# Seven block products instead of eight in the down projection of 29 of 64 groups

## The chip, the cores and the metric

The kernel runs on one core of one Trainium2 chip. The metric is device time in microseconds of one execution of the whole program; a version's time is the median of its runs. The engines are named as the profile names them: PE is TensorE (PEld its weight loads), DVE is VectorE, ACT is ScalarE, POOL is GpSimd, SP is SyncE, which only issues transfers here.

## The reference

Two layers of gated cross attention and feed-forward act on x of 2 x 1024 tokens with 256 features. The part that the change touches is the feed-forward part of the first layer, a sum over 8 experts of a gated MLP with 1024 hidden features:

```
x = x + tanh(g_xattn[0]) * attention(layernorm(x), ctx, ctx, W, b)
def expert_step(acc, w):
    wg, wu, wd = w
    h = silu(x @ wg) * (x @ wu)        # x: 2048 x 256, wg and wu: 256 x 1024
    return acc + h @ wd                # wd: 1024 x 256
x = x + tanh(g_ffn[0]) * scan(expert_step, 0, (Wg, Wu, Wd))(layernorm(x))
x = x + tanh(g_xattn[1]) * masked_attention(layernorm(x), ctx, mask, ...)
x = x + tanh(g_ffn[1]) * routed_experts(layernorm(x), ...)
```

All tensors are float32. The second attention has 8 heads, and the last layer sends each token to one of 8 experts with 256 places each.

## The kernel before

The feed-forward stage takes the time from about 75 to 1044 us of a span of 1275 us. Before it stands the first attention, behind it the second attention and the routed experts.

**Tiling.** The 8 x 1024 hidden features are cut into 32 quarters of 256 features, the 2048 tokens into two pairs of chunks of 2 x 512 tokens. A group is one quarter for one pair of chunks, so there are 64 groups. From group 4 on the even groups (pair 0) and the odd groups (pair 1) alternate on the same quarter's weights. Everything is kept transposed: features on the 128 partitions, 512 tokens along the row. A group is thus a product of matrices of 2 x 2 blocks: two blocks of 128 features by two chunks of 512 tokens.

**Gate and up.** For each of the two, the 2 x 2 block product is done by seven block products in place of eight (Strassen and Winograd's form): `product1` to `product7`, with sums of weight blocks and of activation blocks made ahead of time. The weight sums are made by POOL for each quarter in `split_hi` and `split_lo`.

**Three matmuls for one product.** Every block product keeps nearly float32 accuracy by splitting both factors into a high part, rounded to the format that PE reads in one pass, and a low part, the rest. `three` (three matmuls, L1124 to L1126) does high x high, low x high and high x low. The activation's high parts are copies on ACT (`hi_part`, L821), the low parts subtractions on DVE (`lo_part`, L1742). The down weights are split by POOL (`split`, L546 and L548).

**Down.** A group's hidden blocks are called 11, 12, 21, 22 (feature block, chunk). `down(n, part)` has eight parts, each a `three`; two parts accumulate in one bank and form a turn, and DVE adds each of the four turns to the running sum `acc` in SBUF (`add_up`, L1756). So a group has 14 + 8 = 22 block products, 66 matmuls, and four additions.

**Order.** The order is written out by hand on each engine. PE runs in iteration n the 14 products of group n and, between them, the parts of `down` for group n-1, and part 7 of group n-2. DVE's loop has for each group four sums that complete gate and up (`sum_22`, `sum_12`), four products silu(gate) x up (`hid_psum` L1725 and `hid_sum` L1734: the names hid11, hid21, hid22, hid12), four low parts and four additions, 16 instructions. `hid_sum` and `lo_part` read two operands in SBUF, the others one in PSUM and one in SBUF. ACT copies halves out of PSUM, does the silu and the high parts, 14 instructions. POOL does once per quarter, so once per two groups, the ten instructions that split gate and up weights (L516 to L540) and two for the down weights; it starts on a quarter when the last product of the group before (`p4_ps["u"]`) has set the buffers free. SP reloads raw weights behind POOL.

## Time and profile before

| | us |
|---|---|
| median of 3 runs | 1281.11 |
| lowest, highest | 1277.74, 1281.66 |
| the profiled execution's own time | 1277.14 |
| span of its profile | 1275.4 |
| PE busy in the span | 1248.7 |
| DVE busy | 908.1 |
| ACT busy | 643.5 |
| POOL busy | 557.7 |

Busy times are sums over instructions with overlaps taken out. One matmul is shown with 0.39 us, but matmuls are pipelined: the distance of two starts is what one costs. On DVE the distance of two starts in a row is likewise shorter than what one instruction is shown with. A row of the timeline that merges several instructions (x2, x4) gives the time from the start of the first to the end of the last.

### The profile page before, as it was taken

To read this page: it belongs to the slowest core of one execution; us is meant where nothing else is said; L and a number is where in the kernel's file an instruction comes from. 1 tells how busy PE (TensorE), PEld (TensorE's weight loads), DVE (VectorE), ACT (ScalarE), POOL (GpSimd) and SP (SyncE) were. 2 spreads that over 40 slices of the span, in tenths; PEclk is the share of its full clock that TensorE was granted. 3 is DMA by queue.
4 is the path that set the end of the run, shared out by engine and by line. 5 is a ranking of instruction groups with operands and counts; after the bars stand their busy time and mean duration, and the time that the engine had idled before them with its cause. 6 is when DMAs were issued, how large, how long until landed. Compare 5 with 4: busy or idle time off the path is not lost.

```text
span 1275.4 us, 17854 instructions
## 1 busy us (share of the span) xinstructions
PE 1248.7 (98%) x6236; PEld 1008.2 (79%) x6236; DVE 908.1 (71%) x1663; ACT 643.5 (50%) x1369; POOL 557.7 (44%) x545
## 2 busy tenths in 40 slices
PE   7999999999999999999999999999999999999998
PEld 5778888888888888888888888888888877787775
DVE  5897767777777677777777777777777775677546
ACT  2465554554555555545445555555554445545543
POOL 3644654444444444444444444444444016544435
PEclk9999999999999999999999999999999999999999
DMA  4100300000000000011000000000000130000131
GB/s 136 47 4 1 117 26 25 25 26 25 25 25 25 25 25 25 26 37 39 25 26 25 26 25 25 26 25 26 26 25 1 50 116 1 18 22 15 34 96 62
DMA packets 41640, 44.04 MB, mean 35 GB/s; under 512 B 4159, under 2 KB 40063, under 8 KB 41423
## 3 DMA queue, kind: packets, MB, share of 16 engines
...
## 4 chain that ended last, share of the span: by engine, by line
PE 90%; DVE 4%; ACT 3%; issue 1%; POOL 1%; DMA 0%; POOLq 0%; ACTq 0%; DVEq 0%
PE bank L1125 26%; PE bank L1124 26%; PE bank L1126 25%; ACT PC L867 2%; PE bank L1338 2%; PE bank L1329 2%; PE bank L1491 1%; PE bank L1508 1%; DVE nmC L1812 1%; PE bank L1441 1%; PE bank L1313 1%; PE bank L1263 1%; PE bank L1268 1%; PE bank L1264 1%; PE bank L1030 1%
## 5 line engine op out<-in xcount | busy, mean ns | idle before, releaser
L1124 PE MATMUL bank<-xop_hi,w_hi 128*128 128x512 f32 x896 | 350.9, 392 | 1.2 <-ACT half_g L798 1.2
L1125 PE MATMUL bank<-xop_lo,w_hi 128*128 128x512 f32 x896 | 351.7, 393 | 0.0
L1126 PE MATMUL bank<-xop_hi,w_lo 128*128 128x512 f32 x896 | 350.9, 392 | 0.0
L1756 DVE TENSOR_TENSOR acc<-bank,acc 128x512 f32<-128x512 f32 x248 | 170.9, 689 | 119.7 <-PE bank L1126 119.5
L1742 DVE TENSOR_TENSOR hid_lo<-hid,hid_hi 128x512 fp32r<-128x512 f32 x256 | 213.8, 856 | 34.7 <-ACT hid_hi L821 34.6
L1124 PE MATMUL bank<-hid_hi,wd_hi 128*128 128x512 f32 x512 | 202.5, 395 | 0.6 <-DVE hid_lo L1742 0.6
L1125 PE MATMUL bank<-hid_lo,wd_hi 128*128 128x512 f32 x512 | 203.0, 396 | 0.0
L1124 PEld LDWEIGHTS bank<-xop_hi,w_hi 128*128 128x128 f32 x896 | 168.2, 188 | 42.2 <-ACT half_g L798 1.5
L1126 PE MATMUL bank<-hid_hi,wd_lo 128*128 128x512 f32 x512 | 201.4, 393 | 0.0
L1125 PEld LDWEIGHTS bank<-xop_lo,w_hi 128*128 128x128 f32 x896 | 168.2, 188 | 38.3
L1126 PEld LDWEIGHTS bank<-xop_hi,w_lo 128*128 128x128 f32 x896 | 168.1, 188 | 37.3
L806 ACT ACTIVATE s<-bank 128x512 f32<-128x512 f32 x128 | 78.1, 611 | 176.1 <-PE bank L1126 176.1
L821 ACT CAST hid_hi<-hid 128x512 fp32r<-128x512 f32 x256 | 157.8, 624 | 1.9 <-DVE hid L1734 1.9
L782 ACT COPY bank<-bank 128x512 f32<-128x512 f32 x128 | 73.0, 570 | 123.5 <-PE bank L1126 123.5
L516 POOL TENSOR_TENSOR w_raw<-raw_gu 128x256 f32<-128x256 f32 x32 | 24.1, 753 | 250.3 <-PE bank L1126 250.3
L546 POOL CAST wd_hi<-raw_d 128x512 fp32r<-128x512 f32 x32 | 19.6, 613 | 234.3 <-PE bank L1126 234.3
L1126 PEld LDWEIGHTS bank<-hid_hi,wd_lo 128*128 128x128 f32 x512 | 96.4, 188 | 22.8
L1124 PEld LDWEIGHTS bank<-hid_hi,wd_hi 128*128 128x128 f32 x512 | 96.1, 188 | 22.9 <-DVE hid_lo L1742 1.0
L1125 PEld LDWEIGHTS bank<-hid_lo,wd_hi 128*128 128x128 f32 x512 | 96.0, 187 | 21.1
L1725 DVE TENSOR_TENSOR hid<-bank,s 128x512 f32<-128x512 f32 x128 | 87.8, 686 | 19.7 <-PE bank L1126 19.7
L812 ACT ACTIVATE half_g<-half_g 128x512 f32<-128x512 f32 x128 | 81.2, 635 | 20.6 <-DVE half_g L1715 19.5
L536 POOL TENSOR_TENSOR w_lo<-w_raw,w_hi 128x1024 fp32r<-128x1024 f32 x32 | 86.5, 2704 | 4.0 <-DVE xnA L1578 1.6
...
## 6 DMA issues: line engine op xcount, KB each, us to landing
...
slots<-empty_row SPq DMA_DIRECT2D x1, 2080.0 KB, 10.8
...
x_res<-in_x_dram SPq DMA_DIRECT2D x4, 512.0 KB, 5.1
...
out_dram<-x_res SPq DMA_DIRECT2D x3, 512.0 KB
```

The lines of the kernel that those rows point to most:

```text
L536: nc.gpsimd.tensor_tensor(out=lo[:, :, W_S1:W_S4 + 1], in0=s[:, :, W_S1:W_S4 + 1], in1=hi[:, :, W_S1:W_S4 + 1].bitcast(F32), op=ALU.subtract)
L782: nc.scalar.copy(bank[FORK_BANK[X]][:], bank[SUM_BANK[X]][:]).then_inc(forked[X], 1)
L806: nc.scalar.activation(out[:], ps[:], ACT.Silu).then_inc(silu_ready[h], 1)
L812: nc.scalar.activation(half["g"][:], half["g"][:], ACT.Silu).then_inc(silu_ready[h], 1)
L821: nc.scalar.copy(hid_hi[n % 2][h][:], hid[h][:]).then_inc(hi_ready[h], 1)
L867: ins = nc.scalar.activation(PC[j % 2][:, h, :], bank[SIM[h // HH * 2 + h % 2]][:, a * KEYS:(a + 1) * KEYS], ACT.Exp, bias=nmC[j % 2][:, h ...
L1124: mm(ps, w, a, start=start, stop=False, skip_group_check=True)
L1125: mm(ps, w, a_low, start=False, stop=False, skip_group_check=True)
L1126: return mm(ps, w_low, a, start=False, stop=True, skip_group_check=True)
L1725: nc.vector.tensor_tensor(out=hid[h][:], in0=ps[:], in1=s[:], op=ALU.mult).then_inc(hid_ready[h], 1)
L1742: nc.vector.tensor_tensor(out=hid_lo[n % 2][h][:], in0=hid[h][:], in1=hid_hi[n % 2][h][:].bitcast(F32), op=ALU.subtract).then_inc(lo_ready ...
L1756: nc.vector.tensor_tensor(out=to, in0=ps, in1=to, op=ALU.add).then_inc(acc_added, 1)
```

## The change

In 29 groups (pair 0, quarters 2 to 30: groups 4, 6, ... 60) the down projection is also done by seven block products, called M1 to M7 by the kernel. For that:

- POOL makes for each such quarter four sums of 128 x 128 blocks of the down weights and splits them (`split_down_sums`: six instructions, put ahead of `split_hi`), and for each such group four sums of hidden blocks T3, T1, T2, T4 (`hid_sums`: four 128 x 512 subtractions, put between `split_lo` and `split_down`). `split_down_sums` waits for the sixth product of the group two before.
- ACT makes the high parts of 11, 21, 22 and of the four T, seven instead of four; DVE makes as many low parts, and adds seven products instead of four turns: M2, M3 and M4 to blocks of `acc`, M1, M5, M6 and M7 to accumulators of their own.
- PE does each M as one `three` into one bank, so 21 matmuls instead of 24, in the order M1, M3, M2, M7, M5, M6, M4, in the places of `down`'s parts; one place (step 4) stays empty. M4 stands in the next iteration, as part 7 did.
- Once, after group 60, POOL joins the four accumulators into `acc` by eight additions (`join_products`), before DVE may add group 62.
- The new tiles lie where x_res (the residual, 16 KB per partition) was. x_res is therefore written to DRAM (x_mid) once, early in the stage, and read back in four transfers after group 60; the residual additions wait for them.

The diff, cut to its core (`add_up`, `hi_part`, `lo_part` and the waits on counters are otherwise adapted to the new counts by `turns_before` and `splits`):

```diff
+        def seven(n):
+            return inside(n) and pair(n) == 0 and 2 <= quarter(n) <= NQ - 2
+        def turns(n):
+            return len(M_ORDER) if seven(n) else 4
+        def turns_before(n):
+            return sum(turns(m) for m in range(n))
+        def sevens_before(n):
+            return sum(seven(m) for m in range(n))
+        def splits(n, h):
+            return n + 1 - (sevens_before(n + 1) if h == "12" else 0)
+        M_ORDER = ("M1", "M3", "M2", "M7", "M5", "M6", "M4")
+        T_ORDER = ("T3", "T1", "T2", "T4")
...
+                if q == 2:
+                    sp.wait_ge(a_ln2, NC)
+                    sp.dma_start(x_mid, x_res[:]).then_inc(x_kept, 16)
...
+            def split_down_sums(q):
+                d, S1, S2, S3, S4 = raw_d[q % 2], 0, 1, 2, 3
+                f0, f1 = slice(0, P), slice(P, 2 * P)
+                if q == 2:
+                    pool.wait_ge(x_kept, X_KEPT + 16)
+                else:
+                    pool.wait_ge(down_ps, turns_before(PAIRS * (q - 1)) + M_ORDER.index("M6") + 1)
+                nc.gpsimd.tensor_tensor(out=wds_raw[:, S1], in0=d[:, 0, f1], in1=d[:, 1, f1], op=ALU.add)
+                own_step(nc.gpsimd.tensor_tensor(out=wds_raw[:, S3], in0=d[:, 0, f0], in1=d[:, 0, f1], op=ALU.subtract))
+                own_wait()
+                own_step(nc.gpsimd.tensor_tensor(out=wds_raw[:, S2], in0=wds_raw[:, S1], in1=d[:, 0, f0], op=ALU.subtract))
+                own_wait()
+                own_step(nc.gpsimd.tensor_tensor(out=wds_raw[:, S4], in0=d[:, 1, f0], in1=wds_raw[:, S2], op=ALU.subtract))
+                own_wait()
+                own_step(nc.gpsimd.tensor_copy(wds_hi[:], wds_raw[:]))
+                own_wait()
+                nc.gpsimd.tensor_tensor(out=wds_lo[:], in0=wds_raw[:], in1=wds_hi[:].bitcast(F32),
+                                        op=ALU.subtract).then_inc(wds_ready, 1)
+            def hid_sums(n):
+                k = len(T_ORDER) * sevens_before(n)
+                pool.wait_ge(down_ps, turns_before(n - 1))
+                pool.wait_ge(hid_ready["22"], n + 1)
+                pool.wait_ge(hid_ready["12"], n + 1)
+                nc.gpsimd.tensor_tensor(out=t_raw["T3"][:], in0=hid["22"][:], in1=hid["12"][:], op=ALU.subtract).then_inc(t_ready, 1)
+                nc.gpsimd.tensor_tensor(out=t_raw["T1"][:], in0=hid["12"][:], in1=hid["11"][:], op=ALU.subtract).then_inc(t_ready, 1)
+                pool.wait_ge(t_ready, k + 2)
+                nc.gpsimd.tensor_tensor(out=t_raw["T2"][:], in0=hid["22"][:], in1=t_raw["T1"][:], op=ALU.subtract).then_inc(t_ready, 1)
+                pool.wait_ge(t_ready, k + 3)
+                pool.wait_ge(hid_ready["21"], n + 1)
+                nc.gpsimd.tensor_tensor(out=t_raw["T4"][:], in0=hid["21"][:], in1=t_raw["T2"][:], op=ALU.subtract).then_inc(t_ready, 1)
+            def join_products(n):
+                c11, c12 = (acc[:, 0, t * CH:(t + 1) * CH] for t in range(2))
+                c21, c22 = (acc[:, 1, t * CH:(t + 1) * CH] for t in range(2))
+                m1, m5, m6, m7 = (m_acc[i][:] for i in ("M1", "M5", "M6", "M7"))
+                def add(to, a):
+                    return nc.gpsimd.tensor_tensor(out=to, in0=to, in1=a, op=ALU.add)
+                pool.wait_ge(acc_added, turns_before(n + 1))
+                own_step(add(m6, m1))
+                add(c11, m1)
+                own_wait()
+                add(m7, m6)
+                own_step(add(c12, m6))
+                own_wait()
+                add(c21, m7)
+                own_step(add(c22, m7))
+                own_wait()
+                add(c12, m5)
+                add(c22, m5).then_inc(joined, 1)
...
             for q in range(2, NQ):
-                split(q)
+                n = PAIRS * (q - 1)
+                if seven(n):
+                    split_down_sums(q - 1)
+                split_hi(q)
+                split_lo(q)
+                if seven(n):
+                    hid_sums(n)
+                split_down(q)
+            join_products(n)
...
+            def t_hi_part(n, i):
+                if not seven(n):
+                    return
+                act.wait_ge(t_ready, len(T_ORDER) * sevens_before(n) + T_ORDER.index(i) + 1)
+                nc.scalar.copy(t_hi[i][:], t_raw[i][:]).then_inc(t_hi_ready, 1)
             for n in range(GROUPS + 1):
                 fork(n, "g")
@@ -826,13 +958,20 @@
                 fork(n, "u")
                 if n == 0:
                     x_raw_out(2)
+                if seven(n - 1):
+                    hi_part(n - 1, "21")
+                    t_hi_part(n - 1, "T3")
                 keep_u2(n, "g")
-                hi_part(n - 1, "21")
+                if not seven(n - 1):
+                    hi_part(n - 1, "21")
+                t_hi_part(n - 1, "T1")
                 if n == 1:
                     x_hi_first(1)
                 keep_p5(n, "g")
                 keep_p5(n, "u")
+                t_hi_part(n - 1, "T2")
                 silu_psum(n, "11", s11, bank[SUM_BANK["g"]], p2_ps)
+                t_hi_part(n - 1, "T4")
...
+            def down_seven(n, m):
+                i, turn = quarter(n) % 2, turns_before(n) + M_ORDER.index(m)
+                whole_hi, whole_lo = wd_hi[i][:], wd_lo[i][:]
+                f0, f1 = slice(0, P), slice(P, 2 * P)
+                own, at = (hid_hi[n % 2], hid_lo[n % 2]), (t_hi, t_lo)
+                w, w_low, (hi, lo), h = {
+                    "M1": (whole_hi[:, 0, f0], whole_lo[:, 0, f0], own, "11"),
+                    "M2": (whole_hi[:, 1, f0], whole_lo[:, 1, f0], own, "21"),
+                    "M3": (wds_hi[:, 3], wds_lo[:, 3], own, "22"),
+                    "M4": (whole_hi[:, 1, f1], whole_lo[:, 1, f1], at, "T4"),
+                    "M5": (wds_hi[:, 0], wds_lo[:, 0], at, "T1"),
+                    "M6": (wds_hi[:, 1], wds_lo[:, 1], at, "T2"),
+                    "M7": (wds_hi[:, 2], wds_lo[:, 2], at, "T3")}[m]
+                if m == "M1":
+                    pe.wait_ge(wds_ready, sevens_before(n) + 1)
+                    pe.wait_ge(lo_ready["11"], splits(n, "11"))
+                elif m == "M6":
+                    pe.wait_ge(t_lo_ready, T_LO_READY + len(T_ORDER) * sevens_before(n) + T_ORDER.index("T2") + 1)
+                else:
+                    pe.wait_ge(acc_added, turn - 1)
+                three(bank[DOWN_BANK[turn % 2]][:], w, w_low, hi[h][:], lo[h][:], True).then_inc(down_ps, 1)
...
+            def down_step(n, step):
+                if not seven(n):
+                    down(n, step)
+                elif step != 4:
+                    down_seven(n, M_ORDER[step if step < 4 else step - 1])
...
+            def t_lo_part(n, i):
+                dve.wait_ge(t_hi_ready, T_HI + len(T_ORDER) * sevens_before(n) + T_ORDER.index(i) + 1)
+                if i in ("T1", "T2"):
+                    dve.wait_ge(t_ready, len(T_ORDER) * sevens_before(n) + T_ORDER.index(i) + 2)
+                nc.vector.tensor_tensor(out=t_lo[i][:], in0=t_raw[i][:], in1=t_hi[i][:].bitcast(F32),
+                                        op=ALU.subtract).then_inc(t_lo_ready, 1)
...
+                if n == GROUPS - 2 and part == 0:
+                    dve.wait_ge(joined, JOINED + 1)
...
+            def add_seven(n, m):
+                turn = turns_before(n) + M_ORDER.index(m)
+                own_block = {"M2": (0, 0), "M3": (0, 1), "M4": (1, 0)}
+                f, t = own_block.get(m, (0, 0))
+                to = acc[:, f, t * CH:(t + 1) * CH] if m in own_block else m_acc[m][:]
+                ps = bank[DOWN_BANK[turn % 2]][:]
+                dve.wait_ge(down_ps, turn + 1)
+                if m not in own_block and sevens_before(n) == 0:
+                    nc.vector.tensor_copy(to, ps).then_inc(acc_added, 1)
+                else:
+                    nc.vector.tensor_tensor(out=to, in0=ps, in1=to, op=ALU.add).then_inc(acc_added, 1)
...
+                if seven(n):
+                    group_of_seven(n)
+                elif seven(n - 1):
+                    group_behind_seven(n)
+                else:
+                    group(n)
```

DVE, around the end of an even group and the start of the odd one behind it. Names: hidXY are the products silu(gate) x up, hid_lo their low parts, half22 and half12 the sums that complete gate and up, acc the running sum, m_acc the new accumulators. Before:

```order
L1742 TENSOR_TENSOR hid_lo12_0_132<-hid12_126,hid_hi12_0_128 128x512
L1742 TENSOR_TENSOR hid_lo22_0_134<-hid22_165,hid_hi22_0_130 128x512
L1756 TENSOR_TENSOR acc_143<-bank7,acc_143 128x512
L1742 TENSOR_TENSOR hid_lo11_0_131<-hid11_125,hid_hi11_0_127 128x512
L1742 TENSOR_TENSOR hid_lo21_0_133<-hid21_164,hid_hi21_0_129 128x512
L1756 TENSOR_TENSOR acc_143<-bank6,acc_143 128x512
L1707 TENSOR_TENSOR half22_g_123<-bank1,half22_g_123 128x512
L1715 TENSOR_TENSOR half12_g_121<-bank2,half12_g_121 128x512
L1725 TENSOR_TENSOR hid11_125<-bank3,s11_119 128x512
```

Between the low part of block 21 and the first sum of the next group stood one addition. The same place now, for a group of seven (hid_lo12_0 holds the low part of T3 here):

```order
L1911 TENSOR_TENSOR hid_lo11_0_131<-hid11_125,hid_hi11_0_127 128x512
L1935 TENSOR_TENSOR acc_159<-bank7,acc_159 128x512
L1911 TENSOR_TENSOR hid_lo21_0_133<-hid21_180,hid_hi21_0_129 128x512
L1919 TENSOR_TENSOR hid_lo12_0_132<-t_rawT3_155,hid_hi12_0_128 128x512
L1948 TENSOR_TENSOR m_accM1_156<-bank6,m_accM1_156 128x512
L1919 TENSOR_TENSOR t_loT1_148<-t_rawT1_147,t_hiT1_146 128x512
L1876 TENSOR_TENSOR half22_g_123<-bank1,half22_g_123 128x512
L1948 TENSOR_TENSOR acc_159<-bank7,acc_159 128x512
L1884 TENSOR_TENSOR half12_g_121<-bank2,half12_g_121 128x512
L1894 TENSOR_TENSOR hid11_125<-bank3,s11_119 128x512
L1948 TENSOR_TENSOR acc_159<-bank6,acc_159 128x512
```

Two more instructions stand ahead of the first sum of the next group, and additions of products stand between the sums; over the two groups DVE has 38 instructions where it had 32.

POOL, once per quarter, from the first instruction for the weights of a quarter on. Before:

```order
L516 TENSOR_TENSOR w_raw0_151<-raw_gu0_160 128x2x128
L517 TENSOR_TENSOR w_raw0_151<-raw_gu0_160 128x2x128
L519 CAST w_hi0_150<-raw_gu0_160 128x2x256
L521 TENSOR_TENSOR w_raw0_151<-w_raw0_151,raw_gu0_160 128x2x128
L523 CAST w_hi0_150<-raw_gu0_160 128x2x128
L525 TENSOR_TENSOR w_raw0_151<-raw_gu0_160,w_raw0_151 128x2x128
L528 CAST w_hi0_150<-w_raw0_151 128x2x512
L536 TENSOR_TENSOR w_lo0_152<-w_raw0_151,w_hi0_150 128x2x512
L538 TENSOR_TENSOR w_lo0_152<-raw_gu0_160,w_hi0_150 128x2x256
L540 TENSOR_TENSOR w_lo0_152<-raw_gu0_160,w_hi0_150 128x2x128
L546 CAST wd_hi0_153<-raw_d0_162 128x512
L548 TENSOR_TENSOR wd_lo0_154<-raw_d0_162,wd_hi0_153 128x512
```

After the change the sums of the down weights stand ahead of L516's successor (L571), and after the last of the ten:

```order
L621 TENSOR_TENSOR wds_raw_144<-raw_d1_179,wds_raw_144 128x128
L623 CAST wds_hi_143<-wds_raw_144 128x512
L625 TENSOR_TENSOR wds_lo_145<-wds_raw_144,wds_hi_143 128x512
L571 TENSOR_TENSOR w_raw0_167<-raw_gu0_176 128x2x128
...
L592 TENSOR_TENSOR w_lo0_168<-raw_gu0_176,w_hi0_166 128x2x128
L634 TENSOR_TENSOR t_rawT3_155<-hid22_181,hid12_126 128x512
L635 TENSOR_TENSOR t_rawT1_147<-hid12_126,hid11_125 128x512
L637 TENSOR_TENSOR t_rawT2_150<-hid22_181,t_rawT1_147 128x512
L640 TENSOR_TENSOR t_rawT4_153<-hid21_180,t_rawT2_150 128x512
L603 CAST wd_hi0_169<-raw_d0_178 128x512
```

POOL has 22 instructions per quarter instead of 12, and the T sums, which the hidden blocks of the same group must wait for, stand behind 16 of them.

## Rows read from the trace of the kernel before

**Rows 1.** The page: busy times and shares, and the chain that ended last.
```profile
span 1275.4 us, 17854 instructions
PE 1248.7 (98%) x6236; PEld 1008.2 (79%) x6236; DVE 908.1 (71%) x1663; ACT 643.5 (50%) x1369; POOL 557.7 (44%) x545
PE 90%; DVE 4%; ACT 3%; issue 1%; POOL 1%; DMA 0%; POOLq 0%; ACTq 0%; DVEq 0%
```

**Rows 2.** Timeline of PE (start us, us): the first matmul of two even iterations.
```profile
610.75 0.39 PE L1124 MATMUL bank<-xop_hi,w_hi 128*128 128x512 f32 x1
...
641.21 0.39 PE L1124 MATMUL bank<-xop_hi,w_hi 128*128 128x512 f32 x1
```

**Rows 3.** Busy time by stretch: PE, PEld, DVE, ACT, POOL, clock, DMA share, GB/s.
```profile
610.75:641.22 30.47, 30.47 (x134) 24.79 (x133) 21.97 (x33) 15.50 (x28) 13.22 (x13) 1.00 0.08 27
1044.00:1275.40 231.40, 217.60 (x1715) 171.40 (x1713) 145.77 (x477) 116.18 (x393) 105.91 (x94) 1.00 0.12 41
```

**Rows 4.** Who waited for whom in the span: us in total, times, longest.
```profile
POOL w_raw L516 <- PE bank L1126: 250.3, 29, 8.7
POOL wd_hi L546 <- PE bank L1126: 234.3, 29, 8.3
```

**Rows 5.** Timeline of DVE in an odd iteration and the even one behind it.
```profile
608.04 0.68 DVE L1715 TENSOR_TENSOR half_u<-bank,half_u 128x512 f32<-128x512 f32 x1
608.64 1.28 DVE L1734 TENSOR_TENSOR hid<-half_u,half_g 128x512 f32<-128x512 f32 x2
...
623.28 0.68 DVE L1715 TENSOR_TENSOR half_u<-bank,half_u 128x512 f32<-128x512 f32 x1
```

**Rows 6.** Timeline of POOL in quarters 3 and 4.
```profile
129.34 1.19 POOL L516 TENSOR_TENSOR w_raw<-raw_gu 128x256 f32<-128x256 f32 x1
130.49 0.74 POOL L517 TENSOR_TENSOR w_raw<-raw_gu 128x256 f32<-128x256 f32 x1
131.18 0.61 POOL L519 CAST w_hi<-raw_gu 128x512 fp32r<-128x512 f32 x1
...
134.72 2.40 POOL L536 TENSOR_TENSOR w_lo<-w_raw,w_hi 128x1024 fp32r<-128x1024 f32 x1
137.08 1.74 POOL L538 TENSOR_TENSOR w_lo<-raw_gu,w_hi 128x512 fp32r<-128x512 f32 x1
138.78 1.19 POOL L540 TENSOR_TENSOR w_lo<-raw_gu,w_hi 128x256 fp32r<-128x256 f32 x1
...
176.37 1.30 POOL L548 TENSOR_TENSOR wd_lo<-raw_d,wd_hi 128x512 fp32r<-128x512 f32 x1
```

**Rows 7.** Timeline of DVE in the same and an earlier stretch.
```profile
80.41 6.13 DVE L1742 TENSOR_TENSOR hid_lo<-hid,hid_hi 128x512 fp32r<-128x512 f32 x4
...
95.17 3.05 DVE L1742 TENSOR_TENSOR hid_lo<-hid,hid_hi 128x512 fp32r<-128x512 f32 x2 [1.57 <-ACT hid_hi L821]
...
136.41 2.96 DVE L1734 TENSOR_TENSOR hid<-half_u,half_g 128x512 f32<-128x512 f32 x2
139.29 0.68 DVE L1725 TENSOR_TENSOR hid<-bank,s 128x512 f32<-128x512 f32 x1
```

**Rows 8.** POOL's float32 subtractions of 128x512 beside them, merged.
```profile
78.44 7.55 POOL L380 TENSOR_TENSOR xop_raw<-xop_raw 128x512 f32<-128x512 f32 x4 [3.79 <-ACT xop_raw L731]
```

**Rows 9.** Groups by line: busy us, mean ns, idle before.
```profile
L1742 DVE TENSOR_TENSOR hid_lo<-hid,hid_hi 128x512 fp32r<-128x512 f32 x256 | 213.8, 856 | 34.7 <-ACT hid_hi L821 34.6
L821 ACT CAST hid_hi<-hid 128x512 fp32r<-128x512 f32 x256 | 157.8, 624 | 1.9 <-DVE hid L1734 1.9
L546 POOL CAST wd_hi<-raw_d 128x512 fp32r<-128x512 f32 x32 | 19.6, 613 | 234.3 <-PE bank L1126 234.3
```

**Rows 10.** The line of the low parts: duration ns min/median/max.
```profile
L1742 DVE TENSOR_TENSOR hid_lo<-hid,hid_hi x256: 672/684/1786, 80.4 to 1040.4; 128x512 fp32r<-128x512 f32 x128
```

**Rows 11.** DMA issues of the page: KB each, us to landing.
```profile
slots<-empty_row SPq DMA_DIRECT2D x1, 2080.0 KB, 10.8
x_res<-in_x_dram SPq DMA_DIRECT2D x4, 512.0 KB, 5.1
```

167 lines of the change are left out of this document (122 added, 45 removed).

## The prediction, made before the change was timed

> **What bounds the kernel now.** I read the page first: PE is busy in 98% of the span and holds 90% of the chain that ended last, DVE is at 71%, POOL at 44% [rows 1]. Then the timeline of PE: two iterations (an even group and the odd one behind it, a pair from here on) take 641.21 - 610.75 = 30.46 us for 132 matmuls, 0.2308 us each and 0.692 us for a `three`, with no gap [rows 2]. The windows say what else a pair holds: DVE 21.97 us, ACT 15.50, POOL 13.22, clock 1.00 [rows 3]. So PE bounds the stage and a matmul taken away is time gained, as long as nobody else needs more than PE. The waits show the slack of POOL, 17 us per pair: 8.6 before a quarter's first sum and 8.1 before the down weights [rows 4]. DVE has 30.5 - 22.0 = 8.5 us of slack. The last view is the timeline of DVE beside that of POOL, because the change loads just these two, and there stands what decides.
>
> A DVE instruction of 128x512 costs 0.60 us in a row (608.04 to 608.64), and two hid products 1.28 [rows 5]. With POOL at work beside them it is otherwise. The same two products took 2.96 us at 136.41: POOL was in L536 from 134.72 to 137.12; the first product waited for its end, then POOL's L538, shown with 1.74 us instead of the 1.30 of a free 128x512 subtraction, waited 0.45 for the product, and the second product waited for L538 [rows 6, 7]. They alternate, an instruction of the one for an instruction of the other. Four low parts beside POOL's subtractions took 6.13 us, 1.53 each, and two took 3.05 [rows 7]. The instruction with one operand in PSUM at 139.29 took 0.68, undisturbed [rows 7], though POOL's L540 ran from 138.78 to 139.97 [rows 6]. So only DVE instructions with two SBUF operands (low parts and the hid products of blocks 22 and 12) and POOL's stand in each other's way. Before, POOL rests 17 of 30 us, and the 256 low parts have a mean of 0.856 against a median of 0.684 [rows 9, 10].
>
> The Trainium skill (SBUF, State Buffer, "Who interferes with whom") calls this an exclusive lock on a port pair shared by DVE and GpSimd, held for the whole instruction, not a split of bandwidth. By that rule POOL's added work is not absorbed by overlap, which speaks against this change; if the two shared smoothly, the sum would come out as the first rival below. The rows at 136.41 and 137.08 agree with the lock.
>
> **The change part by part.**
>
> PE loses 3 matmuls in 29 pairs: 0.692 each pair, 20.1 us in all; a pair would take 29.77.
>
> ACT gets 3 copies more per pair, 3 x 0.624 = 1.9 us [rows 9] on 15.5: hidden, since it keeps 12 us of rest; the places where it waits for POOL's sums are below.
>
> DVE gets 6 instructions more per pair: 38 x 0.605 = 23.0 us free of disturbance. Of its two-SBUF-operand instructions there are now 15 (4 hid, 7 + 4 low parts), where there were 12.
>
> POOL gets per pair: four sums of 128x128 weights. No row has this form; from 128x256 (0.69 from start to start) and 128x512 (1.25), both free [rows 6], the slope gives 0.41 each, by the nearest rows between 0.2 and 0.74. I take 0.41, with 0.13 for three of them that wait for their own predecessor: 2.0. A cast 0.69 with its wait, a low part 1.27: together 4.0. Four T sums of 128x512 at 1.27 and 0.08 for two waits: 5.3. So 22.5 us instead of 13.2, and more than that with waits for DVE at 0.45 to 0.5 each.
>
> Now the order. I place one pair in its steady state, time 0 being PE's first matmul of the even iteration n.
>
> POOL. It is released 0.3 us after M6 of the former pair, the last product of the odd iteration. Free work up to the end of T1: weight sums 4.0; the ten split instructions 9.3 (134.72 - 129.34 = 5.4 up to L536, less 0.45 of waiting in the first of them, 137.08 - 134.72 = 2.4 for L536, 1.25 and 0.74 for the last two [rows 6]); T3 and T1 1.27 each: 15.8. On the way nine DVE instructions with two SBUF operands cut in (hid22 and hid12, four low parts of the odd group before; hid22, hid12 and low part 22 of the new one), at 0.49 each: 4.4. T1 ends at 0.3 + 15.8 + 4.4 = 20.5, or 20.7 with the short rests between them.
>
> DVE. At the start low part 12 of the odd group meets the low part of the weight sums (1.0), and PE, which wants it at 4.9, is 0.9 late from there. hid22, due at 13.1 (it follows the sum at 623.28, 0.60 later; 623.88 - 610.75 [rows 2, 5]), thus comes at 14.1, in POOL's L536 (0.5); hid12 meets L538 as at 136.41 (1.2), low part 22 meets T3 (0.7), low part 11 meets T1 (1.2) and starts at 20.7. M1, PE's eighth `three` of the odd iteration, wants low part 11 at 15.23 + 4.85 + 0.9 = 21.0 and gets it at 21.4. From 20.7 to the end of the low part of T2 DVE has 14 instructions (low 11, addition, low 21, low T3, M1, low T1, sum, M3, sum, hid11, M2, sum, M7, low T2): 8.5 us, plus 0.7 that low 21 waits for T2 and 1.2 that low T3 waits for T4: 31.0. M6 wants the low part of T2 at 29.1 without any stall, at 30.5 with the stalls so far, and gets it at 31.0; it ends at 31.7, and its end starts POOL's next round. The ring closes: a pair takes 31.7 us, 1.25 more than before. The same number comes from DVE's account: 38 instructions 23.0, 13 of the 15 disturbed at a mean of 0.64 by this placement 8.3, 0.4 idle: 31.7. DVE is then busy nearly always and is the bound.
>
> Bounds of that disturbance: 0.17 us (856 - 684 [rows 9, 10]) gives 15 x 0.17 = 2.6, DVE 25.6, and PE bounds at 29.77; 0.93 (1.53 - 0.60 [rows 7]) gives 13 x 0.93 = 12.1, a pair of 35.5, 146 us in all. I take 0.64, since half of what stands beside DVE is shorter than a 128x512 subtraction.
>
> The waits that I cost at nothing: POOL's T sums are late for ACT nowhere (T3 ends at about 18.9; ACT is busy until 19.3 with a copy behind PE's product at 18.0 and the high part of 21). The transfer of x to DRAM stands on SP between the loads of quarters 2 and 3; 2 MB took 10.8 us [rows 11], and quarter 3 is wanted at 129 [rows 6], some 40 us after it. Reading back takes four times some 5 us [rows 11], from about iteration 62 on, 30 us before the first residual addition at 1046. The eight joining additions on POOL take 8 x 1.27 and up to eight waits of 0.5, 14 us, from about 8 us in iteration 62 to 7 us in iteration 63, where DVE wants group 62: just hidden, 5 us if not. A new load of raw_d waits for the weight sums, and still has over 20 us.
>
> Sum: 29 x 1.25 = +36 us on the profiled execution's 1277.1, 1313. Its time lies 4 us below the median of the runs, 1281.1, which gives 1317. I say 1315.
>
> **The rivals.**
>
> 1. Faster: DVE keeps up and PE stays the bound. What decides is the stretch from hid22 (13.1) to the low part of T2, which M6 wants at 29.1: 19 instructions of DVE, 11.5 us, so that 16.0 leave 4.5 for seven disturbed ones, 0.64 each. Under that the pair takes 29.8 and the whole gains 20 us: 1261. For it: 10 of the 38 instructions in DVE's new order are PSUM additions that stand between disturbed ones, and if POOL's round runs 2 us earlier than I place it, L536 is over before hid22 and T1 before low part 11. Against it: full alternation costs 0.9 or more and four of the seven (hid12, low 11, low 21, low T3) meet a 128x512 subtraction.
> 2. About the same: half of the disturbance above 0.64, a pair of 30.3 to 30.6.
> 3. Worse: hid22 meets all of L536 (2.4 instead of 0.5), and low part 12 of the odd group stands behind the low part of the weight sums (1.3) so that PE's down parts of the odd group wait too; a pair of 33.3, +82 us, 1360.
> 4. POOL loses more often than in turn. Its first subtraction at 78.44 waited for both hid products: the four took 7.55 us, free they are 5.1 [rows 8], while DVE's two took their free 1.28. If DVE keeps the way over two instructions in a row, hid12 saves 1.2 and POOL is 0.5 later: a pair of about 31.1, 1300. This lies inside my own range.
>
> **How the numbers follow.** My forecast with variant 4, a pair of 30.7 to 32.7: 60%, its own range 1288 to 1345. Rival 1: 27%. Rival 2: 7%. Rival 3: 6%. What a measurement of this kernel can tell from no change is about 0.3%, 4 us. Faster 0.27, same 0.07, slower 0.66. The range from 1260 to 1345 leaves out rival 3 and the lowest part of rival 1.
>
> **What would show it.** Right: DVE busy over 88% of the span; the hid products of 22 and 12 with a mean near 1 us instead of 0.69; PE's idle time, in front of M1 by the low part of 11 and in front of M6 by the low part of T2, some 2 us per pair; starts of the first matmul of even iterations 31 to 33 apart; POOL's first sum of the down weights still waiting for PE, some 4 us. Wrong: pairs of 29.8 with PE without gaps (rival 1), or PE waiting for a T sum through ACT, for the T sums would then be slower than the rows say. 6236 - 87 = 6149 matmuls would show that the change does what it says.

## The result, and the profile after

The changed kernel takes 1296.83 us (median of 4 runs, 1295.74 to 1298.91), the kernel before 1279.42 (4 runs beside it, 1277.22 to 1281.66): a ratio of 1.0132 [1.0112, 1.0153]. It is slower, as forecast, and inside the range, but by 17 us where the forecast had 34 (1315 against 1281.1). The profiled execution took 1295.74.

The page after, answering [rows 1]:

```profile
span 1293.9 us, 18364 instructions
PE 1249.0 (97%) x6149; PEld 986.5 (76%) x6149; DVE 1155.2 (89%) x1837; ACT 695.3 (54%) x1456; POOL 922.4 (71%) x843
PE 63%; DVE 25%; issue 5%; ACT 4%; POOL 2%; DMA 0%; DVEq 0%; POOLq 0%; ACTq 0%
```

87 matmuls are gone, as the change says. DVE went from 71% to 89%, and of the chain that ended last it now holds a quarter. The next line is the stretch from one first gate and up weight sum of POOL to the one 25 pairs later (columns as in [rows 3]).

```profile
227.20:999.80 772.60, 759.63 (x3226) 599.77 (x3225) 761.48 (x951) 431.46 (x776) 637.40 (x551) 1.00 0.08 26
```

By 25: a pair takes 30.90 us (before 30.47 [rows 2]), and in it DVE is busy 30.46, POOL 25.50 (waits for each other's instructions are counted in both), PE 30.39, for 129 matmuls that need 29.77. PE loses 1.13 us a pair. The timeline of PE tells where; 592.50 is the first matmul of the even iteration, 623.41 that of the next one:

```profile
592.50 0.40 PE L1263 MATMUL bank<-xop_hi,w_hi 128*128 128x512 f32 x1
...
613.32 0.47 PE L1263 MATMUL bank<-hid_hi,wd_hi 128*128 128x512 f32 x1 [0.47 <-DVE hid_lo L1911]
...
622.61 0.50 PE L1263 MATMUL bank<-t_hiT,wds_hi 128*128 128x512 f32 x1
...
623.41 0.40 PE L1263 MATMUL bank<-xop_hi,w_hi 128*128 128x512 f32 x1
...
629.64 0.48 PE L1263 MATMUL bank<-hid_hi,wd_hi 128*128 128x512 f32 x1
629.96 0.40 PE L1264 MATMUL bank<-hid_lo,wd_hi 128*128 128x512 f32 x1
```

The row at 613.32 is M1. Measured from start to start, against 0.231 for each matmul, M1 starts 0.62 late and its second step 0.08, M6 (622.61) 0.20 and its second step 0.11, and one step at 629.96, the first that wants the low part of 22 of the odd group, is 0.09 late: 1.10 in all. The waits of 130 to 1010 us say it for all 28 pairs (us in total, times, longest):

```profile
POOL wds_raw L616 <- PE bank L1265: 129.8, 28, 4.7
PE bank L1263 <- DVE hid_lo L1911: 14.0, 28, 0.8
PEld bank L1263 <- DVE t_loT L1919: 13.1, 28, 0.6
PEld bank L1263 <- DVE hid_lo L1911: 6.8, 28, 0.3
```

Both waits of PE are for DVE, for the two instructions that the prediction named, the low part of 11 and a low part of T. Now DVE and POOL beside each other, first the end of the even iteration, then the start of the next:

```profile
603.86 0.69 DVE L1876 TENSOR_TENSOR half_u<-bank,half_u 128x512 f32<-128x512 f32 x1 [0.47 <-PE bank L1265]
...
605.76 3.30 DVE L1903 TENSOR_TENSOR hid<-half_u,half_g 128x512 f32<-128x512 f32 x2
...
610.19 2.99 DVE L1911 TENSOR_TENSOR hid_lo<-hid,hid_hi 128x512 fp32r<-128x512 f32 x2
613.10 0.68 DVE L1935 TENSOR_TENSOR acc<-bank,acc 128x512 f32<-128x512 f32 x1
...
623.68 1.54 DVE L1903 TENSOR_TENSOR hid<-half_u,half_g 128x512 f32<-128x512 f32 x2
...
626.94 2.62 DVE L1911 TENSOR_TENSOR hid_lo<-hid,hid_hi 128x512 fp32r<-128x512 f32 x2
```

```profile
604.40 2.40 POOL L588 TENSOR_TENSOR w_lo<-w_raw,w_hi 128x1024 fp32r<-128x1024 f32 x1
606.77 1.74 POOL L590 TENSOR_TENSOR w_lo<-raw_gu,w_hi 128x512 fp32r<-128x512 f32 x1
608.48 1.18 POOL L592 TENSOR_TENSOR w_lo<-raw_gu,w_hi 128x256 fp32r<-128x256 f32 x1
609.63 1.29 POOL L634 TENSOR_TENSOR t_rawT<-hid,hid 128x512 f32<-128x512 f32 x1
610.88 1.74 POOL L635 TENSOR_TENSOR t_rawT<-hid,hid 128x512 f32<-128x512 f32 x1
...
623.65 1.02 POOL L616 TENSOR_TENSOR wds_raw<-raw_d 128x128 f32<-128x128 f32 x1 [4.73 <-PE bank L1265]
624.64 0.91 POOL L617 TENSOR_TENSOR wds_raw<-raw_d 128x128 f32<-128x128 f32 x1
...
626.70 0.61 POOL L623 CAST wds_hi<-wds_raw 128x512 fp32r<-128x512 f32 x1
627.39 1.63 POOL L625 TENSOR_TENSOR wds_lo<-wds_raw,wds_hi 128x512 fp32r<-128x512 f32 x1
```

I call the time from 603.86 to 613.10 the **stretch**: it begins when PE hands over the u product that closes the sum of block 22, and ends with the low part of 11, for which M1 waits. It holds nine DVE instructions, 5.4 us alone. It took 9.24, since the hid products of 22 and 12 (3.30 instead of 1.2) met L588 and L590 and the low parts of 22 and 11 (2.99 instead of 1.2) met T3 and T1.

Three things outside the steady pairs. The last copy of the first quarter's sums started at 129.82 and the last addition of the stage at 1064.08; in another profiled execution of the kernel before these are 129.31 and 1048.08, in the one that the prediction worked from 126.94 and 1045.71. So the stage grew by 15.5 us: 28 x 0.44 = 12.2, and 3.2 in the first pair with seven products. There M1 waits longer than in the pairs behind it (147.14), and PE waits for ACT twice, which it does in no steady pair:

```profile
147.14 0.47 PE L1263 MATMUL bank<-hid_hi,wd_hi 128*128 128x512 f32 x1 [0.75 <-DVE hid_lo L1911]
...
150.53 0.50 PE L1263 MATMUL bank<-xop_hi,w_hi 128*128 128x512 f32 x1 [1.06 <-ACT half_g L922]
...
154.84 0.50 PE L1263 MATMUL bank<-xop_hi,w_hi 128*128 128x512 f32 x1 [0.58 <-ACT half_u L922]
```

The other 2.9 us of the profiled execution (129.82 against 126.94) lie ahead of the stage. They come from PE's clock and are not the change's. Busy time by stretch, after:

```profile
62.00:67.00 5.00, 5.00 (x13) 4.00 (x12) 4.96 (x11) 2.71 (x5) 0.92 (x1) 0.50 0.00 0
```

the same stretch in the second profiled execution of the kernel before (run b_again below), with one more from behind the stage:

```profile
62.00:67.00 5.00, 5.00 (x13) 4.01 (x12) 4.90 (x13) 2.31 (x5) 0.44 (x1) 0.50 0.19 60
1073.00:1078.00 5.00, 4.01 (x26) 3.08 (x28) 3.35 (x9) 3.64 (x18) 4.73 (x5) 0.66 0.00 0
```

and in the execution behind [rows 1]:

```profile
62.00:67.00 5.00, 5.00 (x24) 4.28 (x23) 4.96 (x11) 3.69 (x8) 1.39 (x1) 1.00 0.41 138
```

The granted clock of this stretch is 0.50, the level of 1.2 GHz, in the first two and 1.00, the level of 2.4 GHz, in the third. So this dip comes in executions of both kernels, and the execution that the prediction worked from was without it. Of the ten runs of before in b_again one had a mean clock of 1.000 and took 1277.4, seven had 0.995 and took 1281.0 to 1281.5. By the two profiled executions of before, 2.4 us of this difference arise ahead of the stage (129.31 against 126.94) and 1.9 behind it, where the clock fell twice more (once within 1073 to 1078, where its mean is 0.66). Two of the four runs of before in the result above took 1277.2 and 1277.7, and no run of the changed kernel had a mean clock of 1.000. The 17 us hold this difference too. What the change costs is the growth of the stage, 15.5 us, and 1296.83 is 15.5 us above the median of b_again, 1281.30. Behind the stage nothing was added: from its last addition to the end of the span it is 229.8 us, before 229.7, so the join and the reload of x are hidden.

### The profile page after: what moved, and what is told of

It reads as the page before. It is cut to its first block, busy times and chain, and to the rows that moved or that the text cites. A ratio compares the mean times of both kernels' runs of the same rounds, so it can differ in the third digit from the quotient of the medians.

```text
span 1293.9 us, 18364 instructions
## 1 busy us (share of the span) xinstructions
PE 1249.0 (97%) x6149; PEld 986.5 (76%) x6149; DVE 1155.2 (89%) x1837; ACT 695.3 (54%) x1456; POOL 922.4 (71%) x843
## 3 DMA queue, kind: packets, MB, share of 16 engines
q0 software_dynamic: 1440, 3.41, 0.7%
## 4 chain that ended last, share of the span: by engine, by line
PE 63%; DVE 25%; issue 5%; ACT 4%; POOL 2%; DMA 0%; DVEq 0%; POOLq 0%; ACTq 0%
PE bank L1263 17%; PE bank L1264 16%; PE bank L1265 16%; DVE hid_lo L1911 7%; DVE hid L1903 6%; ACT PC L1006 2%; DVE acc L1935 2%; DVE hid L1894 2%; DVE half_u L1876 2%; PE bank L1507 2%; DVE half_u L1884 2%; PE bank L1498 2%; PE bank L1660 1%; PE bank L1677 1%; DVE nmC L2056 1%
## 5 line engine op out<-in xcount | busy, mean ns | idle before, releaser
L1911 DVE TENSOR_TENSOR hid_lo<-hid,hid_hi 128x512 fp32r<-128x512 f32 x227 | 271.2, 1228 | 3.3 <-ACT hid_hi L946 3.2
L1263 PE MATMUL bank<-hid_hi,wd_hi 128*128 128x512 f32 x338 | 138.3, 409 | 15.0 <-DVE hid_lo L1911 15.0
L1903 DVE TENSOR_TENSOR hid<-half_u,half_g 128x512 f32<-128x512 f32 x128 | 150.2, 1211 | 0.0
L1264 PE MATMUL bank<-hid_lo,wd_hi 128*128 128x512 f32 x338 | 133.9, 396 | 0.0
L1265 PE MATMUL bank<-hid_hi,wd_lo 128*128 128x512 f32 x338 | 133.1, 394 | 0.0
L616 POOL TENSOR_TENSOR wds_raw<-raw_d 128x128 f32<-128x128 f32 x29 | 29.5, 1018 | 129.8 <-PE bank L1265 129.8
L1263 PEld LDWEIGHTS bank<-hid_hi,wd_hi 128*128 128x128 f32 x338 | 63.4, 187 | 45.9 <-issue 25.9
L1935 DVE TENSOR_TENSOR acc<-bank,acc 128x512 f32<-128x512 f32 x132 | 89.9, 681 | 6.4 <-PE bank L1265 6.3
L588 POOL TENSOR_TENSOR w_lo<-w_raw,w_hi 128x1024 fp32r<-128x1024 f32 x32 | 77.0, 2407 | 4.1 <-DVE xnA L1747 1.6
L720 POOL TENSOR_TENSOR PC<-PC,rdenC 128x616 f32<-128x616 f32 x32 | 38.9, 1215 | 54.0 <-DVE rdenC L2064 54.0
L1948 DVE TENSOR_TENSOR m_accM<-bank,m_accM 128x512 f32<-128x512 f32 x112 | 75.6, 675 | 0.0
```

Source lines behind the costliest of these rows:

```text
L588: nc.gpsimd.tensor_tensor(out=lo[:, :, W_S1:W_S4 + 1], in0=s[:, :, W_S1:W_S4 + 1], in1=hi[:, :, W_S1:W_S4 + 1].bitcast(F32), op=ALU.subtract)
L1263: mm(ps, w, a, start=start, stop=False, skip_group_check=True)
L1264: mm(ps, w, a_low, start=False, stop=False, skip_group_check=True)
L1265: return mm(ps, w_low, a, start=False, stop=True, skip_group_check=True)
L1903: nc.vector.tensor_tensor(out=hid[h][:], in0=half["u"][:], in1=half["g"][:], op=ALU.mult).then_inc(hid_ready[h], 1)
L1911: nc.vector.tensor_tensor(out=hid_lo[n % 2][h][:], in0=hid[h][:], in1=hid_hi[n % 2][h][:].bitcast(F32), op=ALU.subtract).then_inc(lo_ready ...
```

## The experiments

In the table, "pair" is the time of a pair and "DVE busy" DVE's part of it, "first" is the length of the two hid products of the even group, "second" that of its low parts 22 and 11, "stretch" as above, and "late" how much later than 0.231 us behind its predecessor M1 starts. Ratios are to the kernel before, timed beside the kernel in question. e2, e3, e4 and e6 leave out a part of the work, so their down projection is not the reference's.

| kernel | us | ratio | pair | DVE busy | first | second | stretch | late |
|---|---|---|---|---|---|---|---|---|
| changed | 1296.83 | 1.0132 [1.0112, 1.0153] | 30.90 | 30.46 | 3.30 | 2.99 | 9.24 | 0.62 |
| e1_early_sums | 1266.57 | 0.9887 [0.9859, 0.9915] | 29.77 | 28.97 | 2.11 | 2.59 | 7.66 | 0 |
| e2_no_t | 1264.03 | 0.9872 [0.9836, 0.9909] | 29.77 | 28.36 | 3.00 | 1.29 | 7.2 | 0 |
| e3_no_w | 1266.98 | 0.9892 [0.9863, 0.9922] | 29.77 | 26.68 | 1.46 | | | 0 |
| e4_no_tw | 1268.14 | 0.9900 [0.9870, 0.9930] | 29.77 | 26.31 | | | | 0 |
| e6_no_tlow | 1264.23 | 0.9847 [0.9822, 0.9871] | 29.77 | 27.59 | 2.49 | 2.98 | 8.42 | 0 |
| e7_wait_p1 | 1296.95 | 1.0113 [1.0093, 1.0133] | 30.91 | 29.97 | 3.41 | 2.99 | 9.34 | 0.74 |
| e8_wait_m4 | 1332.68 | 1.0386 [1.0366, 1.0407] | 32.18 | 29.89 | 3.97 | 1.83 | 8.74 | 0.13 |
| e9_early_wait_m4 | 1303.15 | 1.0166 [1.0144, 1.0189] | 31.17 | 30.39 | 3.57 | 2.98 | 9.50 | 0.89 |
| e10_two_halves | 1298.03 | 1.0115 [1.0098, 1.0132] | 31.03 | 30.58 | 3.45 | 2.99 | 9.38 | 0.77 |
| e11_one_more | 1298.76 | 1.0121 [1.0105, 1.0138] | 30.92 | 30.47 | 3.34 | 2.50 | 9.27 | 0.67 |
| e12_early_one_more | 1289.83 | 1.0069 [1.0042, 1.0097] | 29.9, 31.5 | 30.00 | | | | 0.26 |
| e13_first_pair | 1265.34 | 0.9876 [0.9855, 0.9897] | 29.83 | 28.90 | | | | |
| e14_early_wait_p1 | 1264.71 | 0.9875 [0.9845, 0.9904] | 29.77 | 28.37 | 2.40 | 2.60 | 7.95 | 0 |

**First: is it POOL's added work, and which?** My theory was that the time over 29.77 comes from POOL's new work beside DVE's and from the late end of its round; the rival that DVE's 38 instructions are too many whatever POOL does.

e1_early_sums moves the four raw weight sums ahead of POOL's wait for M6, into T3's high tile, which is free from M7 on:

```diff
                 if seven(n):
+                    raw_down_sums(q - 1)
                     split_down_sums(q - 1)
...
+                    pool.wait_ge(down_ps, turns_before(PAIRS * (q - 1)) + M_ORDER.index("M7") + 1)
```

> The changed kernel with one edit: GpSimd makes the four raw sums of the down weights as soon as the seventh product's weight (M7) of the group before is read, in the memory of T3's high tile, instead of after M6 together with their split; only the cast and the low part still wait for M6. The same instructions, about 3.3 us of GpSimd's work per pair moved from behind its wait of 4.7 us for TensorE to ahead of it. My theory: what is left over the 129 matmuls of a pair (30.91 against 129 x 0.2308 = 29.77 us) comes from GpSimd's round being late and its instructions lying beside VectorE's in the last third of the pair; then T1 ends 3 us earlier, TensorE no longer waits before M1 and M6, the pair goes to 29.8 to 30.1 us and the time to 1268 to 1275 us. Rival one (VectorE's 38 instructions a pair are the bound, whatever GpSimd does when): no change, 1297 us. Rival two (the same GpSimd work only meets other VectorE instructions): the pair within 0.3 us of 30.9, 1289 to 1305 us.

1266.57: 30 us below the changed kernel and 1.1% below the one before. POOL's low parts now start 1.4 us before the stretch instead of 0.5 behind its start, and DVE's two pairs of instructions in it are 1.6 us shorter:

```profile
617.76 0.69 DVE L1885 TENSOR_TENSOR half_u<-bank,half_u 128x512 f32<-128x512 f32 x1 [0.75 <-PE bank L1274]
...
619.66 2.11 DVE L1912 TENSOR_TENSOR hid<-half_u,half_g 128x512 f32<-128x512 f32 x2
...
622.89 2.59 DVE L1920 TENSOR_TENSOR hid_lo<-hid,hid_hi 128x512 fp32r<-128x512 f32 x2
```

```profile
616.40 2.42 POOL L589 TENSOR_TENSOR w_lo<-w_raw,w_hi 128x1024 fp32r<-128x1024 f32 x1
```

Over 25 pairs PE has no gap left, with DVE still busy 97% of the time, by the same view as for the changed kernel:

```profile
222.70:966.90 744.20, 744.20 (x3227) 603.72 (x3226) 724.28 (x952) 423.96 (x776) 642.40 (x552) 1.00 0.09 27
```

e2, e3 and e4 cut POOL's added work to 8 columns, from the second group with seven products on: the T sums, the weight sums, both. The core of e2:

```diff
+                    out, a, b = t_part[:, k], a[:, 0:8], b[:, 0:8]
+                nc.gpsimd.tensor_tensor(out=out, in0=a, in1=b, op=ALU.subtract).then_inc(t_ready, 1)
```

> The changed kernel with GpSimd's four sums of hidden blocks (T1 to T4) cut to 8 columns from the second seven-product group on; ScalarE and VectorE split the tiles of the first one again at full width, so their counts and widths stay; the down projection's products with T are therefore not those of the reference. Takes some 5 us from GpSimd's round in every pair, from its end, and leaves the weight sums. If GpSimd's work beside VectorE (or its round's length) sets the pair: the wait before M1 goes, pair 29.9 to 30.2 us, 1268 to 1276 us. If VectorE's count of instructions sets it: 1295 to 1298 us.

> The changed kernel with GpSimd's six instructions on the down-weight sums cut to 8 columns from the second seven-product group on (the products take the first one's weight sums, so the down projection is not the reference's). Their order and waits stay. Takes some 4 us from the start of GpSimd's round. If GpSimd's round and its meetings with VectorE set the pair: 29.9 to 30.2 us, 1268 to 1276 us. If VectorE's count sets it: 1295 to 1298 us. If only the hidden sums at the round's end matter and not when they come: about 1297 us here too, with the whole gain in the other cut.

> Both cuts together: the changed kernel with the hidden sums and the down-weight sums of GpSimd cut to 8 columns from the second seven-product group on (the down projection is not the reference's). VectorE keeps its 38 instructions, ScalarE its 29, TensorE its 129 matmuls a pair. If GpSimd's added work is the whole cause of the 1.1 us over TensorE's own time: pair 29.8 us, VectorE's disturbance down from 7.5 to about 5 us a pair as before the change, 1264 to 1270 us, some 12 us below the kernel before. If VectorE's count is the bound: 1290 to 1297 us. A part of the 18 us over the kernel before that stays even with a pair of 29.8 us would lie outside the steady stage.

All four fall to the same pair of 29.77 us, so DVE's count is not the bound, and either half of POOL's addition taken away is enough. The busy time of DVE prices the meetings with all 38 instructions kept (e3, then e4):

```profile
221.50:965.70 744.20, 744.20 (x3227) 605.82 (x3226) 667.12 (x951) 424.79 (x776) 549.83 (x552) 1.00 0.09 27
```

```profile
221.70:965.90 744.20, 744.20 (x3227) 605.80 (x3226) 657.83 (x952) 424.66 (x776) 396.16 (x552) 1.00 0.09 27
```

26.31 us a pair with POOL's added work cut to 8 columns (22.8 alone, 38 x 0.60, so 3.5 of meetings with its old work and the 8-column rests), 0.4 more with the T sums, 2.0 more with the weight sums (e2), but 4.15 more with both and 2.7 with both in e1's order. The same instructions of POOL cost DVE 1.5 us more or less a pair by where they lie.

**Second: which loop closes the pair?** A pair could close on the ring that the prediction drew (M6, POOL's round, T2, its low part, M6), or on DVE. e7 and e8 start POOL's round later, e6 cuts the low parts of T on DVE to 8 columns.

```diff
# e7_wait_p1, behind the wait for M6 (e8_wait_m4: index("M6") + 2 instead, the product M4)
+                    pool.wait_ge(p1_ps["g"], PAIRS * q + 1)
# e6_no_tlow
-                nc.vector.tensor_tensor(out=t_lo[i][:], in0=t_raw[i][:], ...)
+                nc.vector.tensor_tensor(out=t_low[i][:], in0=t_raw[i][:, 0:8], ...)
```

> The changed kernel with VectorE's four low parts of the hidden sums (T1 to T4) cut to 8 columns in every seven-product group; GpSimd's work, its place and every wait stay, and the products take T's high tile in place of the low one (so the down projection is not the reference's). VectorE's 38 full instructions a pair become 34, some 2.2 us less, of which 0.5 to 1.1 us lies in the chain from GpSimd's T2 to M6. If the pair closes on a loop M6 -> GpSimd's round -> T2 -> its low part -> M6, it shortens by the part that lies in the loop, to 30.0 to 30.4 us, 1272 to 1283 us. If VectorE is simply full (it is busy 98% of the steady stage), 2.2 us less is enough for TensorE's own 29.77 us, 1264 to 1268 us. If only GpSimd's work counts: 1295 to 1298 us.

> The changed kernel with GpSimd's weight sums waiting for the first product of the group behind M6 as well: no instruction more on any engine, GpSimd's round merely starts some 0.7 us later in every pair. If the pair closes on the loop M6 -> GpSimd's round -> T2 -> M6, the delay is paid once per pair: 30.91 + 0.7 = 31.6 us, about 1317 us. If VectorE's work with what the shared port adds to it is the bound, it only moves the meetings: 30.7 to 31.2 us, 1291 to 1305 us.

> As before, but the weight sums wait for M4, the seventh product, which TensorE issues 3.5 us after M6. The loop would give 30.91 + 3.4 = 34.3 us a pair, some 1395 us; a VectorE bound about 31 us, 1290 to 1310 us. GpSimd's own round takes about 26 of the 30.9 us, so that from a delay of 4.7 us (its wait now) its own work would bound the pair too, and by less than the loop.

e6 falls to PE's time at once. e7, the ring's own test, should have cost 20 us and costs nothing: some 0.8 us of delay in every pair and the pair is 30.91. My first reading was that DVE is full. But in e7 DVE is idle 0.9 us a pair, twice as much as in the changed kernel, at the same pair. The delay went elsewhere: POOL, starting later, met only the second of DVE's hid products, with its first sum (0.84), and its second sum was free (0.47); in the changed kernel they took 1.02 and 0.91.

```profile
624.12 0.84 POOL L617 TENSOR_TENSOR wds_raw<-raw_d 128x128 f32<-128x128 f32 x1 [5.51 <-PE bank L1266]
624.93 0.47 POOL L618 TENSOR_TENSOR wds_raw<-raw_d 128x128 f32<-128x128 f32 x1
```

The third sum starts 2.4 us behind the start of the pair, in the changed kernel 2.2: of a delay of 0.8 at the first, 0.6 is made up. e8's delay of 3.5 us is not made up: +1.27 a pair, 36 us, far less than the ring's 98, and more than I gave the rival. PE's longest wait is another one there: ACT stands idle 1.9 us for T3, and PE then waits for ACT's copy of u behind it, 0.86 us.

> The kernel before, unchanged, for the granted clock and the span of each of its runs: the changed kernel's profile shows the clock at 0.63 and 0.68 from 60 to 70 us and its steady stage starting 2.9 us later, while the profile of before shows 1.00 there; the times of before so far fall near 1277.5 and near 1281.5 us. If the same dip comes and goes in the kernel before, its slow runs have a mean clock of 0.995 to 0.997 and spans 3 to 4 us above 1275.4, and 2.9 us of the 17 us are in half of the runs of before as well. If not, the dip belongs to the change and all runs here have clock 1.000.

b_again: 1281.30 (10 runs), ratio 0.9994 [0.9981, 1.0006], the profiled one with a clock of 0.995 and a span of 1279.7. The dip is in both kernels (rows above), so the change costs the 15.5 us of the stage and not the 18.5 by which the first two profiled spans differ.

**Third: the stretch.** The table shows that wherever it has both and M1 is late, M1 is late by the stretch less 8.61 us (9.24 - 0.62, 9.34 - 0.74): the 39 matmuls from the u product to M1, 9.00 us, less the hand-over on both sides. I tested this from four sides. The 0.31 us of M6 I did not test by itself.

```diff
# e9_early_wait_m4: e1, with index("M6") + 2 for the cast of the weight sums
# e10_two_halves
-                nc.gpsimd.tensor_tensor(out=lo[:, :, W_S1:W_S4 + 1], ...)
+                for side in range(2):
+                    nc.gpsimd.tensor_tensor(out=lo[:, side, W_S1:W_S4 + 1], ...)
# e11_one_more, and in e1: e12_early_one_more; ahead of hid 21 of a group with seven products
+                    nc.vector.tensor_tensor(out=aside[:], in0=ps[:, 0:416], in1=s[:, 0:416], op=ALU.mult)
```

> The kernel with the early raw weight sums, but the cast and low part of them wait for M4 instead of M6: the same instructions on every engine, and the rest of GpSimd's round some 3.3 us later, so that the low part of the eight weight sums (128x1024, 2.4 us) starts about 2 us after VectorE's first sum of u instead of 1.4 us before it. My theory now: from that sum of u to M1 VectorE has 9 instructions (5.4 us undisturbed) and TensorE 39 matmuls (9.0 us); GpSimd's low parts that lie beside this stretch decide it (9.3 us in the changed kernel with the low part 0.5 us after the sum, 7.7 us in the early one). With the same work put back beside it the stretch is 8.8 to 9.5 us again and the whole gain goes: pair 30.6 to 32.2 us, 1288 to 1333 us. Rival (taking work out from behind the wait is what helps, wherever the rest lies): 1266 to 1272 us.

e9 came as expected: the same instructions as e1, later, and the gain is gone, 1303. The stretch is 9.50 and M1 late by 0.89 = 9.50 - 8.61.

> The changed kernel with one edit: GpSimd's low part of the eight weight sums is written as two instructions of 128x512 (by side) instead of one of 128x1024, so that none of its instructions beside the stretch is longer than 1.3 us. If VectorE gets its turn at the end of each GpSimd instruction, the hidden product that now takes 1.8 us loses up to 1.2 us less, and the pair falls to 29.8 to 30.2 us, 1264 to 1277 us; if the wait is only shared out differently (VectorE waits for the second half as well, in the next instruction), 30.7 to 31.0 us, 1291 to 1300 us.

e10 is no faster, but decides little: hid22 was issued at 606.73 with the second half already running, so that it waited 1.15 for one short instruction where it had waited 1.0 for the rest of the long one.

> The changed kernel with one more VectorE instruction in each seven-product group, 416 columns of the product that makes hidden block 21 written aside (0.48 to 0.5 us, one operand in PSUM), in the stretch between the sum of u and M1. If this stretch is what closes the pair, the instruction is paid one to one: 30.91 + 0.5 = 31.4 us, about 1311 us (28 to 29 pairs). If VectorE had room (it is idle 0.4 us in a pair by the profile, 0.9 us in the kernel with the delayed round at the same pair), 1297 to 1300 us.

e11 was a miss: half a microsecond more of DVE inside the stretch, and the stretch is 9.27 instead of 9.24.

```profile
608.77 0.58 DVE L1896 TENSOR_TENSOR aside<-bank,s 128x416 f32<-128x416 f32 x1
...
610.46 2.50 DVE L1914 TENSOR_TENSOR hid_lo<-hid,hid_hi 128x512 fp32r<-128x512 f32 x2
```

The added instruction reads PSUM, and POOL worked on beside it; the low parts then waited 0.49 less (2.50 for 2.99), since the last of them begins when POOL's T1 ends, whenever it was issued. I read this so: the length of the stretch is set by the ends of POOL's instructions as long as DVE meets them one by one, and the loop of the pair runs through both engines.

> The same added instruction in the kernel with the early raw sums. The stretch is 7.7 us there against the 8.85 us that TensorE's 39 matmuls cover, so 1.1 us are free: the pair stays at 29.77 us and the time at 1266 to 1268 us, although VectorE's busy share of the pair rises from 97% to 99%. If VectorE's total is what counts instead, it has 0.8 us of room and pays for a part only where GpSimd's meetings shift: up to 1272 us.

e12 was the larger miss. In e1 the same instruction costs 23 us, though the stretch alone had 0.95 us of room for it. From one round of POOL to the next it is 29.9 and 31.5 us in turn: in one pair M1 is late by 0.26, in the other M4 waits for DVE's addition.

```profile
639.97 0.47 PE L1273 MATMUL bank<-hid_hi,wd_hi 128*128 128x512 f32 x1
...
653.86 0.50 PE L1273 MATMUL bank<-t_hiT,wd_hi 128*128 128x512 f32 x1 [0.78 <-DVE m_accM L1960]
```

So the stretch before M1 is one place that decides and not the only one. That DVE's total (29.5 of 29.77 with the added instruction) leaves too little for a change of the meetings is my reading, and no run tests it. Why the order flips in every second pair stays open.

**Fourth: what was left.**

```diff
# e13_first_pair, on e1: split_down(2) behind split_down_sums(2) instead of ahead of it,
# and PE's M1 waits for this split as well
# e14_early_wait_p1, on e1: the wait of e7
```

> The kernel with the early raw sums, and for the first pair with seven products GpSimd makes the weight sums and then splits the down weights of that quarter (which waits 8.3 us for TensorE), instead of the other way round. If this wait is what makes T3 3.9 us late for ScalarE there, TensorE's waits before the M1 of that pair and the four behind it (0.93 + 1.22 + 0.76 + 0.42 + 0.20 us, and 0.5 us of longer first steps) go for the greater part: 3 to 4 us, so 1262.5 to 1264 us, with the pair unchanged at 29.77 us. If something else delays T3: 1266 to 1268 us.

> The kernel with the early raw sums, its cast of the weight sums waiting for the first product of the next group too, so 0.4 to 0.7 us later, as in the delayed version of the changed kernel. No work is added. If the pair hangs on where GpSimd's low parts meet VectorE's stretch from the sum of u to M1, the 128x1024 low part starts 0.7 us before that sum instead of 1.4 us, the stretch is 8.0 to 8.9 us of the 8.85 us that are covered, and the pair 29.8 to 30.1 us: 1266 to 1275 us. If the early version only holds in one exact order and any shift throws it out of it, as the added VectorE instruction did, 30.5 to 31 us, 1285 to 1300 us.

e13 took the waits for ACT out of the first pair and left M1 0.28 late for 0.92, which shows that POOL's wait of 8.3 us for PE ahead of the weight sums was their cause. In the pair behind it M4 then waited 0.97, and the pairs are 0.06 longer; the stage is 901.9 us instead of 902.5, and the times of the two (1265.3, 1266.6) can't be told apart. e14 came as expected: 0.7 us later and the pair stays at 29.77, with a stretch of 7.95.

The version that beats both kernels is e1_early_sums, 1266.57 against 1282.21 of the kernel before beside it.

## Why the prediction was right in its direction and wrong in its size

- **PE's saving, 0.692 us a pair**: right. Where nothing holds PE the pair is 29.77 us, in six kernels.
- **DVE's own 23.0 us, 89% busy, POOL's wait of some 4 us for PE** (22.8, 89%, 4.73): right.
- **The alternation of DVE and POOL and the stretch from hid22 to M1**: right. The prediction had 0.5 + 1.2 for the waits of the hid products and 0.7 + 1.2 for those of the low parts, 3.6; the rows have 2.1 + 1.8, 3.9. The runs e1 to e4 show that POOL's added work is the cause, and that the rule of the Trainium skill that the prediction used (SBUF, State Buffer, "Who interferes with whom"), that DVE and POOL lock each other out for a whole instruction, points the right way: each of the two hid products here waited until POOL's L588 or L590 was over, 2.1 us in all.
- **The step that failed: "low part 12 of the odd group meets the low part of the weight sums (1.0), and PE, which wants it at 4.9, is 0.9 late from there."** It was issued 3.53 us into the pair (626.94), while POOL's cast still ran, took 0.91 instead of 0.6 and was done 0.4 us before PE wanted it at 4.85. The low part of the weight sums (627.39) met the next one, low part 22, which PE wants 1.4 us later, and PE was late by 0.09 (629.96). So 0.8 us of this term are missing, while M1 lost 0.70 where the forecast had 0.4 and M6 0.31 where it had 0.5: 1.10 in place of 1.8. M1 starts at 20.8 in the pair, not 21.4 (613.32 - 592.50), M6 at 30.1 instead of 31.0, and the pair is 30.90 instead of 31.7. Over 29 pairs 0.8 us are 23 us, more than the whole miss. POOL was where the forecast had it: its own terms, 0.3 + 2.0 + 0.69 and twice 0.49 for the two hid products, put the low part of the weight sums at 3.97, and the row has 3.98. DVE was earlier: its two hid products at the round's start took 1.54, only 0.3 more than alone, beside two sums that take 0.46 each and were shown with 1.02 and 0.91. What the prediction gave DVE there it does not write out; for the meeting that it names, low part 12 had to be issued after 3.97. Variant 4 had a pair of 31.1 and 1300 us, close to the result, but by another way, with hid12 passing POOL in the stretch; it did not (3.30 for the two), so that this number fits is luck. DVE's disturbance, said to be 8.3, is 30.46 - 22.8 = 7.7.
- **The ring closes on M6 and POOL's round**: too stiff. By it e7 had to cost 20 us and cost nothing. An engine that comes later met less here, and 0.8 us on POOL (e7) or 0.5 on DVE (e11) were given back; 3.3 to 3.5 us were not (e8, e9).
- **All 29 pairs alike**: the first one costs 3.2 us where the steady ones cost 0.44. POOL reaches its weight sums 8.3 us late there (e13); the prediction did not look at the pair in which POOL's order begins.
- **Nothing for the write of x, the reload and the join**: right, no wait of DVE or PE for them.
- **The base**: the profiled execution of before was one without the clock's dip; the forecast met this by half, with 1315 between 1313 and 1317. The 34 us forecast and the 17 measured are therefore not over quite the same base; by the stage alone it is 36 against 15.5.
- **Rival 1** gave the right point of decision: "if POOL's round runs 2 us earlier than I place it" the pair is 29.8. That is e1: L536's successor starts 9.9 us into the pair in place of 11.9 and is over (618.82) before hid22 (619.66). T1, unlike the rival says, was not over before low part 11.
